# Second scan's gate, group norm, layer norm and convolution as one block, with its sums formed in the gate, and constants fetched inside the blocks of other work

## The reference

```python
# third layer, after its scan gave y; z is the other half of the input projection
y = y * jax.nn.gelu(z, approximate=False)
y = y @ W_out
yg = y.reshape(b, GROUPS, -1)
mu = yg.mean(-1, keepdims=True)
var = yg.var(-1, keepdims=True)
yg = (yg - mu) * lax.rsqrt(var + EPS)
y = yg.reshape(b, PAD, h, w) * gn_w[None, :, None, None] + gn_b[None, :, None, None]
x = x + y[:, :c]
# fourth layer
xn = layer_norm(xf, ln_w, ln_b)
chunks = xn.reshape(B, L, 4, dm).transpose(2, 0, 1, 3).reshape(4 * B, L, dm)
xz = chunks @ in_w.T
xi, z = (xz[..., :di], xz[..., di:])
xc = jax.nn.silu(causal_conv(xi, conv_w) + conv_b)   # 4 taps
...                                                   # scan over xc gives y
y = y * jax.nn.silu(z)
ym = y @ out_w.T + skip_scale * chunks
```

## Time and profile before

| | us |
|---|---|
| median of 3 runs | 1867.59 |
| lowest and highest of them | 1861.26, 1868.41 |
| the profiled execution's own time | 1861.92 |
| its span, first to last instruction | 1860.1 |
| scan2's last instruction ends | 1199.6 |
| gate of the third layer, first matmul to last `finish` | 1205.7 to 1226.3 |
| group norm, layer norm, convolution | 1226.5 to 1289.5 |
| scan3's last instruction ends | 1771.7 |
| last gate, first matmul to last `finish` | 1775.2 to 1795.8 |

### The profile page before, as it was taken

The page is one execution under the profiler, slowest core; times in us unless marked ns, Lnnn a source line. Parts: engine busy times, 40 slices in busy tenths (PEclk is TensorE's granted clock), DMA queues, the critical chain, the costliest instruction groups (busy, mean ns, idle before and its releaser), DMA issues. The chain is left out here.

```text
span 1860.1 us, 29105 instructions
## 1 busy us (share of the span) xinstructions
PE 1513.1 (81%) x9958; PEld 776.7 (42%) x9958; DVE 1544.7 (83%) x1256; ACT 1198.4 (64%) x1852; POOL 1081.5 (58%) x702
## 2 busy tenths in 40 slices
PE   6999897998788788788778777568788888878688
PEld 3666545885333333333333333225333333333223
DVE  3778655545899999999999999663899999999955
ACT  5666584335677667766776666367767777776456
POOL 1777401000577777777777777400698999989601
PEclk8999997999899999999999998789899999999989
DMA  4000000000344544454445444400000000000001
GB/s 147 2 0 0 1 1 1 1 1 1 67 93 93 96 93 90 93 96 93 90 92 97 94 90 93 92 0 1 1 1 1 1 0 0 0 0 0 1 13 46
DMA packets 23296, 78.10 MB, mean 42 GB/s; under 512 B 3776, under 2 KB 4672, under 8 KB 22976
## 3 DMA queue, kind: packets, MB, share of 16 engines
q0 software_dynamic: 18288, 66.59, 18.9%
q1 hardware_dynamic: 4944, 10.68, 2.0%
HBM read 8.58 MB, written 2.10 MB: 6 GB/s over the span
## 5 line engine op out<-in xcount | busy, mean ns | idle before, releaser
L1184 POOL TENSOR_TENSOR s_prod<-s_ahead,s_cs 128x1024 f32<-128x1024 f32 x127 | 308.8, 2431 | 185.1 <-DVE s_back L1127 156.3
L2003 POOL TENSOR_TENSOR r_state<-r_state,r_cs 128x1024 f32<-128x1024 f32 x127 | 300.7, 2383 | 120.1 <-ACT r_cs L1889 100.9
L1954 DVE TENSOR_TENSOR_SCAN r_state<-r_decay,r_pu 128x1024 f32<-128x1024 f32 x128 | 292.7, 2287 | 13.7 <-PE r_py L1805 8.7
L1124 DVE TENSOR_TENSOR_SCAN s_ahead<-s_fore,s_pu 128x1024 f32<-128x1024 f32 x128 | 292.7, 2287 | 8.8 <-ACT s_fore L1041 1.8
L1127 DVE TENSOR_TENSOR_SCAN s_back<-s_aft,s_pu 128x1024 f32<-128x1024 f32 x128 | 289.5, 2261 | 1.2 <-ACT s_aft L1051 1.2
L1873 ACT ACTIVATE r_decay<-r_pd,r_aneg 128x1024 f32<-128x1024 f32 x128 | 142.7, 1115 | 101.0 <-PE r_pd L1747 100.6
L1041 ACT ACTIVATE s_fore<-s_pd,s_aneg 128x896 f32<-128x896 f32 x128 | 129.9, 1015 | 112.3 <-PE s_pd L854 111.1
L1747 PE MATMUL r_pu<-r_partsu,selr 64*128 64x512 f32 x512 | 156.3, 425 | 23.3 <-DVE r_state L1954 21.2
L854 PE MATMUL s_pu<-s_partsu,selr 64*128 64x512 f32 x512 | 98.1, 461 | 80.1 <-DVE s_back L1127 76.6
L1950 DVE TENSOR_TENSOR r_pu<-r_pu,r_bs 128x1024 f32<-128x1024 f32 x128 | 154.7, 1208 | 7.7 <-PE r_pu L1747 7.7
L1117 DVE TENSOR_TENSOR s_pu<-s_pu,s_bs 128x1024 f32<-128x1024 f32 x128 | 154.5, 1207 | 3.4 <-PE s_pu L854 3.4
(11 more groups left out here) (355 smaller groups left out, 3266.7 us busy)
## 6 DMA issues: line engine op xcount, KB each, us to landing
s_ahead<-s_back POOLq DMA_DIRECT2D x127, 512.0 KB, 4.5
x_act<-in_x_dram SPq DMA_DIRECT2D x8, 256.0 KB, 5.5
out_dram<-x_act SPq DMA_DIRECT2D x16, 128.0 KB, 2.3
k_fir<-in_pack_fir_dram SPq DMA_DIRECT2D x1, 1600.0 KB, 7.2
k_scan<-in_pack_scan_dram SPq DMA_DIRECT2D x1, 1600.0 KB, 10.6
k_l<-in_pack_l_dram SPq DMA_DIRECT2D x1, 515.0 KB, 4.4
k_l<-in_pack_l_dram SPq DMA_DIRECT2D x1, 450.0 KB, 11.2
k_ln<-in_pack_ln_dram SPq DMA_DIRECT2D x3, 131.0 KB, 3.1
```

The source lines that it names most:

```text
L1124: dve.tensor_tensor_scan(ahead[:, v % 4], f, feed[:], 0.0, ALU.mult, ALU.add).then_inc(ahead_done, 1)
L1184: pool.tensor_tensor(prod[:, b], ahead[:, v % 4], cs[:, buf].rearrange("p i n -> p (i n)"), ALU.mult).then_inc(prod_done, 1)
L1954: dve.tensor_tensor_scan(state[:, v % 4], decay[:, v % 4], feed[:], 0.0, ALU.mult, ALU.add).then_inc(scanned, 1)
L2003: pool.tensor_tensor(state[:, v % 4], state[:, v % 4], cs[:, phase, q // 2], ALU.mult).then_inc(multiplied, 1)
```

## The change

The gate of the third layer and `normed_convolve3` become one block, `gated_convolve3`. Inside the gate, VectorE's `finish` of every second chunk is followed by the sum of its pair (`total`, 128x1); TensorE averages it behind the product `wo` of a later chunk (`mean` on TensorE), and VectorE makes that pair's mean. ScalarE takes the square of pair 0 behind its gate 9 and that of pair 1 behind its gate 13 (counted from 0, two gates a chunk), and the squares of pairs 2 and 3 behind the table load that follows the gates. `scaled` and the add to `x` go in chunks of 512: ScalarE makes the first four, GpSimd the last four, VectorE adds four before the layer norm and one after each of the layer norm's first four chunks. TensorE's banks `ps_z` and `ps_o` are those of the layer norm (`center`, `var`).

The group "l2post" is fetched at the kernel's start, behind "l2". The groups "l3conv", "ln" and "l3" are fetched by SyncE at the start of `gated_convolve3`, "l3post" at the start of `scan3` into the tile that held "l2post", and "ln" and "mlp3" at the start of the last gate. The three blocks of `fetch` are gone. `wz` is stored once for each half in one block of 128 columns, so that both groups have 322 columns instead of 450. The tile of "l2post" is now reserved for the whole program, ahead of all tiles that are reserved later.

```diff
-    "l2post": [("wz", 2 * P), ("wo", C), ("gavg", P), ("gnw", 1), ("gnb", 1)],
+    "l2post": [("wz", P), ("wo", C), ("gavg", P), ("gnw", 1), ("gnb", 1)],
...
-def gated(nc, consts, tag, group, src, y, func, dst, sums=None):
+def gated(nc, consts, dram, tiles, tag, group, src, y, func, dst):
...
+        @block.sync
+        def _(sp):
+            for name, tile in tiles.items():
+                sp.dma_start(tile[:], dram["pack_" + name]).then_inc(consts[name][1], 16)
...
-                        mm = pe.matmul(ps_z[2 * k % 4 + h][:], c["wz"][rows, h * P:(h + 1) * P],
+                        mm = pe.matmul(ps_z[2 * k % 4 + h][:], c["wz"][rows],
...
-def normed_convolve3(nc, consts, src, sums, x, xn, xc):
+def gated_convolve3(nc, consts, dram, tiles, x, y, src, xn):
...
+            for name in ("l3conv", "ln", "l3"):
+                sp.dma_start(tiles[name][:], dram["pack_" + name]).then_inc(consts[name][1], 16)
...
+            def mean(bl):
+                pe.wait_ge(total_done, bl + 1)
+                wait(pe, mean_done, bl)
+                pe.matmul(ps_m[:, bl:bl + 1], g["gavg"], total[:, bl:bl + 1], start=True, stop=True).then_inc(mean_ps, 1)
+
+            for k in range(CHUNKS + 1):
+                if k < CHUNKS:
+                    wait(pe, gate_done, 2 * k - 2)
+                    for h in range(HALVES):
+                        rows = slice(h * C, (h + 1) * C)
+                        mm = pe.matmul(ps_z[2 * k % 4 + h][:], g["wz"][rows], x[rows, k * N:(k + 1) * N],
+                                       start=True, stop=True, tile_position=(h * C, 0))
+                    mm.then_inc(z_done, 2)
+                if k >= 1:
+                    n = k - 1
+                    pe.wait_ge(gy_done, 2 * k)
+                    wait(pe, dst_done, n - 1)
+                    for h in range(HALVES):
+                        mm = pe.matmul(ps_o[n % 2][h * C:(h + 1) * C], g["wo"], gated_y[:, n % 2, h], start=True,
+                                       stop=True, tile_position=(0, h * C))
+                    mm.then_inc(o_done, 1)
+                    if n >= 3 and n % 2 == 1:
+                        mean(n // 2 - 1)
+            mean(BL - 1)
...
-                    pe.wait_ge(x_done, n * N // HW + 1)
+                    pe.wait_ge(x_done, n + 1)
...
+            def spread_square(bl):
+                act.wait_ge(mean_done, bl + 1)
+                wait(act, square_done, bl)
+                act.activation(spread[:], src[:, bl * HW:(bl + 1) * HW], ACT.Square, bias=means[:, bl:bl + 1],
+                               accum_out=var_sum[:, bl:bl + 1]).then_inc(square_done, 1)
+
+            for k in range(2 * CHUNKS):
+                act.wait_ge(z_done, k + 1)
+                wait(act, gy_done, k - 3)
+                act.activation(gate[:, k % 4], ps_z[k % 4][:], ACT.Gelu).then_inc(gate_done, 1)
+                if k >= 9 and k % 4 == 1:
+                    spread_square(k // 4 - 2)
             act.preload_act_table_set("natural_log_exp_and_others")
-            act.wait_ge(mean_done, 1)
-            for bl in range(BL):
-                act.activation(scaled[:, bl], src[:, bl * HW:(bl + 1) * HW], ACT.Square, bias=means[:, bl:bl + 1],
-                               accum_out=var_sum[:, bl:bl + 1]).then_inc(square_done, 1)
+            spread_square(BL - 2)
+            spread_square(BL - 1)
...
-            for bl in range(2):
-                act.activation(scaled[:, bl], src[:, bl * HW:(bl + 1) * HW], ACT.Identity,
...
-            pairs = sums.rearrange("p (b k) -> p k b", k=HW // N)
-            dve.tensor_tensor(total[:], pairs[:, 0], pairs[:, 1], ALU.add).then_inc(total_done, 1)
-            dve.wait_ge(mean_ps, 1)
-            dve.tensor_scalar(means[:], ps_m, -1.0 / HW, None, ALU.mult).then_inc(mean_done, 1)
+            def finish(n):
+                dve.wait_ge(o_done, n + 1)
+                dve.tensor_scalar(src[:, n * N:(n + 1) * N], ps_o[n % 2][:], 1.0, 0.0, ALU.mult, ALU.add,
+                                  accum_out=sums[:, n:n + 1]).then_inc(dst_done, 1)
+                if n % 2 == 1:
+                    bl = n // 2
+                    dve.wait_ge(dst_done, n + 1)
+                    dve.tensor_tensor(total[:, bl:bl + 1], sums[:, n - 1:n], sums[:, n:n + 1],
+                                      ALU.add).then_inc(total_done, 1)
+
+            def mean(bl):
+                dve.wait_ge(mean_ps, bl + 1)
+                dve.tensor_scalar(means[:, bl:bl + 1], ps_m[:, bl:bl + 1], -1.0 / HW, None,
+                                  ALU.mult).then_inc(mean_done, 1)
+
+            for n in range(CHUNKS):
+                for h in range(HALVES):
+                    k = 2 * n + h
+                    dve.wait_ge(gate_done, k + 1)
+                    wait(dve, o_done, n - 1)
+                    dve.tensor_tensor(gated_y[:, n % 2, h], y[:, h, n * N:(n + 1) * N], gate[:, k % 4],
+                                      ALU.mult).then_inc(gy_done, 1)
+                if n >= 1:
+                    finish(n - 1)
+                if n >= 4 and n % 2 == 0:
+                    mean(n // 2 - 2)
+            finish(CHUNKS - 1)
+            mean(BL - 2)
+            mean(BL - 1)
...
-            def add(bl):
-                if bl < 2:
-                    dve.wait_ge(scaled_done, bl + 1)
+            def add(n):
+                if n < CHUNKS // 2:
+                    dve.wait_ge(scaled_done, n + 1)
                 else:
-                    dve.wait_ge(scaled_late, bl - 1)
-                cols = slice(bl * HW, (bl + 1) * HW)
-                dve.tensor_tensor(x[:, cols], x[:, cols], scaled[:, bl], ALU.add).then_inc(x_done, 1)
+                    dve.wait_ge(scaled_late, n + 1 - CHUNKS // 2)
+                cols = slice(n * N, (n + 1) * N)
+                dve.tensor_tensor(x[:, cols], x[:, cols], scaled[:, n], ALU.add).then_inc(x_done, 1)
...
-                if n in (1, 2):
-                    add(n + 1)
+                if n < CHUNKS // 2:
+                    add(n + CHUNKS // 2)
...
-            pool.wait_ge(square_done, BL)
-            for bl in range(2, BL):
-                pool.tensor_scalar(scaled[:, bl], src[:, bl * HW:(bl + 1) * HW], gain[:, bl:bl + 1],
+            for n in range(CHUNKS // 2, CHUNKS):
+                bl = n * N // HW
...
+            sp.dma_start(post_tile[:], dram["pack_l3post"]).then_inc(consts["l3post"][1], 16)
...
+        for group in ("mlp0", "fir", "scan", "l2", "l2post"):
...
+        post, post_tiles = reserve(nc, kept, ["l2post"])
...
+        at, _ = layout(CONST["l3post"])
+        post3 = {"l3post": ({name: post_tiles["l2post"][:, lo:hi] for name, (lo, hi) in at.items()}, m.sem("k_l3post_in"))}
         with ExitStack() as scan_consts:
-            consts = fetch(nc, scan_consts, dram, ["l3"])
+            consts, tiles = reserve(nc, scan_consts, ["l3"])
+            consts = consts | post | post3
             with ExitStack() as first_consts:
-                consts |= fetch(nc, first_consts, dram, ["l2post", "ln", "l3conv"], "3")
+                first, first_tiles = reserve(nc, first_consts, ["l3conv", "ln"], "3")
+                consts, tiles = consts | first, tiles | first_tiles
                 with nc.cleanup_on_exit(), ExitStack() as layer:
-                    mem = Scope(nc, layer)
-                    mixed, sums = mem.sb("mixed2", [P, COLS]), mem.sb("chunk_sums", [P, CHUNKS])
-                    gated(nc, consts, "o2", "l2post", x, y, ACT.Gelu, mixed, sums)
-                    normed_convolve3(nc, consts, mixed, sums, x, xn, y)
-
-            scan3(nc, consts, y[:].rearrange("p h n -> p (h n)"), selr, ysel)
+                    mixed = Scope(nc, layer).sb("mixed2", [P, COLS])
+                    gated_convolve3(nc, consts, dram, tiles, x, y, mixed, xn)
+
+            scan3(nc, consts, dram, post_tiles["l2post"], y[:].rearrange("p h n -> p (h n)"), selr, ysel)
         mixed = m.sb("mixed3", [P, COLS])
-        consts = fetch(nc, kept, dram, ["l3post", "ln", "mlp3"], "4")
-        gated(nc, consts, "o3", "l3post", xn, y, ACT.Silu, mixed)
+        last, last_tiles = reserve(nc, kept, ["ln", "mlp3"], "4")
+        consts = post3 | last
+        gated(nc, consts, dram, last_tiles, "o3", "l3post", xn, y, ACT.Silu, mixed)
         consts["mlp3"][0].update(consts["l3post"][0])
         normed_mlp(nc, consts, "m3", "mlp3", mixed, xn, "lnw", "lnb", x, mixed, out)
```

40 lines of the change are left out of this document (23 added, 17 removed).

## The result

| | before | after |
|---|---|---|
| median, us | 1868.0 | 1852.3 |
| lowest and highest, us | 1861.26, 1868.84 | 1850.41, 1853.88 |
| runs | 4 | 4 |
| the profiled execution's own time, us | 1861.92 | 1850.41 |
| its span, us | 1860.1 | 1848.6 |

The ratio of after to before is 0.9929, with a 95% interval of 0.9903 to 0.9956: faster by 0.7%. A repetition with more runs gave 0.9939 (0.9916 to 0.9962). The medians are 15.7 us apart, while the ratio makes the saving 13.3 us.

What follows compares the result with a forecast made beforehand. VectorE (83%) and TensorE (81%) are busy mostly in the unchanged scans; time is lost at entries, group norm and layer norm. From 1867.6 us, -5.1 + 1.1 - 3.3 - 3.1 = -10.4 gives 1857.2, range 1847 to 1863.

Steps and rivals of the forecast that it cites:

- The entry of the second gate: Between second scan and second gate: with "l2post" loaded early, the first matmul waits for the block alone; -5.1 us.
- The sums inside the gate: Second gate to variance matmul: squares waiting for means delay the last gates 4.35 us, a shorter tail follows; +1.1 us.
- Chunks of 512: Layer norm's start: first centering 1.15 us earlier, the 2.1 us wait before the fifth chunk gone; -3.3 us.
- The last gate: Entry behind the third scan: with weights loaded under that scan, TensorE starts with the block; -3.1 us.
- The sum: Whole kernel: the four terms together, two entries, gate sums and chunks; -10.4 us.
- all ends together: Whole kernel: the saving with every term at its low or high end, between 5.5 and 14.8 us.
- the forecast: Whole kernel: a saving of 8 to 13 us, time 1857.2 us; chance 0.56.
- rival (b): Whole kernel: all clock phases fall well and squares cost only their own time; saving 13 to 15 us, 1853.5; chance 0.13.
- Rival (a): Second gate gives back more through full waits for means and lost clock; saving 5.5 to 8 us, 1860.5; chance 0.22.
- Rival (c): Gate entries not shorter, something the DMA covers holds the first matmul; 1865.4 us; chance 0.05.
- rival (d): Second scan: moved tiles make accumulating DMAs land late, kernel slower than before, 1877 at 0.16 us each; chance 0.04.

Runs made afterwards that it cites:

- after_third: The changed kernel, unchanged, in its third profile; a single run of 1854.4 us.
- e2_squares_late: The changed kernel with all four group norm squares behind the gates' table load, sums and means still in the gate; ratio to the kernel before 0.9935.
- before_third: The kernel before, unchanged, in its third profile; one run of 1860.8 us.
- before_again: The kernel before, unchanged, in its second profile; one run of 1867.0 us.
- e7_l3post_late: The changed kernel with the DMA of "l3post" at the last gate's start instead of the third scan's start; ratio to the kernel before 0.9945.
- e6_resident: The kernel before with "l2post" alone loaded at the start and kept, `wz` in one block, the three blocks of `fetch` staying; ratio 0.9986.
- e1_entries: The kernel before with only the new fetching and `wz` in one block; gate, group norm and chunks as before; 1863.4 us, ratio 0.9974.
- e5_best: The changed kernel with pair 0's square behind gate 11, the others behind the table load, squares writing into `scaled`, pair 2's mean one chunk earlier; 1851.7 us, 0.9909.
- e3_chunks: The kernel before with only `scaled` and VectorE's adds in steps of 512 columns instead of 1024; 1859.8 us, ratio 0.9968.

## Why the prediction was right, and where it was off

**The entry of the second gate**, -5.1 us: right. It measured -4.9 to the first matmul, with 1.03 us where the third scan's entry had given 0.93. The prediction kept 0.9 us more as its lower end, for first matmuls at the higher clock level. That came true in two of three profiles of after, and in none of before: another -0.6 on average. With the new fetching six of eight profiles have it, of the other five none. In before a stretch at the higher level passes by during the long entry; the short one can catch it, and whether it does differs between executions of one kernel (after, after_third).

**The sums inside the gate**, +1.1 us: the mechanism was right, the size too large; it measured +0.1. The first square waited 1.74 us (1.9 expected), and the last gates came 18.1 us after the first (some 19 expected). The mis-sized term is VectorE's catching up between the two squares, "its 1.9 us a chunk", which as laid out there came to 2.0. Its products start at 1213.69 and 1215.51, 1.82 us apart, and a pair's sum and mean, 0.16 and 0.15 us long, start only 0.08 us apart (1211.67 and 1211.75), so that from the first gates behind the first square to those behind the second it was 5.77 us and not 6.3. The first square's own delay was 0.4 us less than laid out. The tail was 6.7 to 7.1 us, 6.8 expected; in the first profile of after the clock was at its lower level from 1221.4 on (0.50), one of the ends that the prediction names. TensorE's averages, which the prediction doesn't price, lie beside ScalarE's waits here; where those waits are gone, in e2_squares_late, they cost 0.6 us.

**Chunks of 512**, -3.3 us: right in both places. The start is 0.96 us earlier (1.15 expected), and the pause of 2.1 us is gone. It measured -4.1 in all, of which 3.1 stand behind the first centering, where 2.1 were expected. The pause itself was priced rightly: with a late rise only its 2.08 us are lost, as in before and before_third. The mis-sized term is the rise of the clock, which the sum leaves at the 6 us of before's first profile and only the range moves. In after it came 5.4, 3.9 and 4.4 us behind the first centering. A pair of matmuls takes 1.91 us before the rise and 1.02 behind it, so by my estimate an earlier rise saves about half of the time by which it is earlier: 0.3, 1.1 and 0.8 us. Before's 21.40 less the pause's 2.08 and less these gives 19.0, 18.3 and 18.5, where 18.89, 18.16 and 18.39 were measured. Before_again had such an early rise too and lost its gain behind the pause (22.00 us). Whether the change makes the rise earlier, or it fell so by chance, the runs don't show. The prediction also had the fifth chunk's add out "about 1 us before TensorE asks for it"; it ends 0.07 us ahead.

**The last gate**, -3.1 us: right, -3.2. Against e7_l3post_late, where only the DMA's place differs, it is 2.2 us, since the landing was faster there.

**The sum**, -10.4 us: the stretches give -13.0, within the 5.5 to 14.8 of all ends together, and on the border of the forecast (8 to 13) and rival (b) (13 to 15). The largest end is 6.0 + 1.0 + 4.6 + 3.1 = 14.7, not 14.8, which changes nothing in the range. Of the 2.6 us by which the stretches exceed the sum, 0.9 is the gate, 0.8 the layer norm, 0.4 the second entry with the clock's level, and 0.4 the last two stretches, which is spread. Rival (a) is out: the gate gave back less than forecast (+0.1), not more. Of rival (b) the clock's half came true, at the second entry and in the layer norm. Its other half did not: two squares at their own time would make the last gates 2.3 us later, and they came 3.4 us later. The measured 1852.3 is nearer to its 1853.5 than to the forecast's 1857, and some of that is luck: the medians' 15.7 us lie outside even the largest end, and a repetition gave 11.4. Rival (c) is out by the entries of 1.03 and 0.33 us, rival (d) by the length of the second scan.

**The base.** The prediction took the median of the runs as base and not the profiled execution, which lay at their lower end. With more runs before stayed at 1867.4 to 1868.6 in the median, so that was right.

## What to carry to other kernels

A block that only issues DMAs looks free, since no engine computes in it, but between two stages it stands on the path of all of them: look at each entry for who is released by a DMA, and move the issue under the stage before. Work put into the gaps of a tight pipeline is free only where its operand is ready when its turn comes: two squares at their earliest places cost the gate what they saved behind it, one square two gates later cost it nothing that the profile shows. And where repeated profiles differ by more than an edit is worth, cut them at the same instructions and compare stretches.

## What the runs showed of the hardware

In these traces the entry of a block takes 0.33 us behind a plain one (last gate of after) and 0.93 to 1.03 behind one that clears semaphores (third scan of before, second gate of after). Two blocks that only issue one or two DMAs added 1.94 us, about 1 us each (2.97 in e6_resident, 1.03 in after).

A table load is 1.28 us long, and the next activation starts 0.01 us behind it (1199.48, 1200.77 in after). Behind the last gate, which ends at 1218.85 + 1.06 = 1219.91, the load starts at 1219.93. The Trainium skill (ScalarE: Activation LUTs, What ACT_TABLE_LOAD costs) adds a drain of 1.38 us to a switch; no trace here shows one, ahead of the load or behind it.

Of two small instructions on VectorE that don't need each other, 0.16 and 0.15 us long, the second starts 0.08 us behind the first (1211.67 and 1211.75 in after).

A pause of TensorE of 2.07 us was followed by 4.4 us in which pairs of matmuls took up to 1.91 us instead of 1.02 (before_again); the granted clock had risen early there, as in e1_entries and e6_resident, and where it rose 6.0 us after the start it stayed at 1.00 behind the same pause (before, before_third). The rise of the clock after the layer norm's start came 2.8 to 6.0 us after its first matmul over all thirteen profiles (earliest in e2_squares_late and e5_best), and TensorE had no pause until then.

From the issue of a DMA of "l3post" at the last gate to its landing it took 2.24 us (e7_l3post_late, 322 columns), 2.46 (e3_chunks, 450), 3.02 (e6_resident, 322) and 3.13 to 3.42 (before, 450).
